# Feed-forward product turned by a DMA instead of by TensorE, in a quantised attention and feed-forward kernel

## The chip, the cores and the metric

The kernel runs on one core of a Trainium2 chip. The metric is the device time of one execution in microseconds (us). A core has five engines with instruction streams of their own: PE (TensorE, matrix products into PSUM banks), DVE (VectorE), ACT (ScalarE), POOL (GpSimd) and SP (SyncE, which here only issues DMAs). Sixteen DMA engines move data between DRAM and SBUF. The engines wait for one another through semaphores, and each works through its own stream in order.

## The reference

Input x and a context, both [64, 128, 256] in float32, go through four residual layers: a gated-memory attention, a ternary linear layer, a softmax cross-attention, and a quantised feed-forward layer. Only the last is touched. For each row of 256 values:

```python
def _act_quant(x):
    scale = 127.0 / clip(max(abs(x), axis=-1), 1e-5)
    return clip(round(x * scale), -128, 127) / scale
def _bitlinear(x, w):                       # w: ternary weights times their mean
    return einsum('bsi,oi->bso', _act_quant(x), _weight_quant(w))
gate = silu(_bitlinear(x, w_gate))          # 256 -> 1024
up = _bitlinear(x, w_up)                    # 256 -> 1024
x = x + _bitlinear(gate * up, w_down)       # 1024 -> 256
```

So the product `gate * up` (128 rows by 1024 of a block) has to be scaled by its row's maximum, rounded to whole numbers up to 127, and turned so that the 1024 inner values lie on the partitions, where the last matrix product sums over them.

## The kernel before

The batch is 64 blocks of 128 rows, in 16 groups (`NG`) of four. The first three layers run as a software pipeline over the groups, whose order is written out by hand in `turn` and `schedule`; the change doesn't touch it. The feed-forward layer follows as a stage of its own over the 64 blocks, with loops unrolled in the program and an order by hand: `ffn_turn` on each engine says what it does for which block in which turn. Its input rows were quantised earlier, stored to DRAM (`rows_q`), and come back turned: SP issues one transposing DMA for each block (`rows_turned`, 128 rows by 256 in bf16), four blocks ahead, as soon as the up product of a block is in its bank.

In turn i of that stage:

- PE makes the gate and up products of block i (`gate_up`, 8 matmuls of 512 columns), turns the rounded product of block i-2 (`product_rows`, 8 transposes), and makes the down product of block i-3 (`down`, 8 matmuls of 256 columns).
- ACT takes silu of the gate banks (`silu`), copies the turned product of block i-2 from PSUM to `fhT` (`product_t`), and scales the down product of block i-3 (`scale_out`).
- DVE multiplies up and silu (`ffn_mul`, the tile `C`), takes the row maximum (`hmax`), guards and scales it (`hstep7`), and inverts it (`hscale`).
- POOL makes the factor for the way back (`scale_back`), rounds the product by adding a large constant (`ffn_round`, tile `wtmp`; the whole number then stands in the low 16 bits), and adds the residual (`ffn_out`).
- SP issues `rows_turned` of block i+4, and for every group one store of 512 KB and one load of 512 KB.

Beside this, `last_rows` on ACT, DVE and POOL normalises and quantises the input rows of the last groups during turns 1 to 46.

Of the kernel before, what the change touches and what calls it, by code (L numbers as in the profile page):

```python
# [5 lines left out]
P = 128  # L6
B = 64
E = 256
# [3 lines left out]
GB = 4  # L12
NG = B // GB
INNER = 1024
# [8 lines left out]
OFFSET = 1536.0  # L23
CODE = 8388608.0 + 0x6600

# [89 lines left out]
def build(nc, x, ctx_in, ig_w, ig_b, fg_w, fg_b, out_w, w0, wq, wkv, w_gate, w_up, w_down, out):  # L115
    rows_q = nc.dram_tensor("rows_q", [B, P, E], BF16, kind="Internal").ap()
    with ExitStack() as ctx:
# [179 lines left out]
        fh = flat(C).rearrange("p (i n) -> p i n", i=2)  # L297
        fhr = flat(wtmp).rearrange("p (i n) -> p i n", i=2)
        fhr_low = fhr.bitcast(F16).rearrange("p i (n w) -> p i n w", w=2)[:, :, :, 0]
# [3 lines left out]
        hstep7 = sb("hstep7", [P, FB])  # L303
        hscale = sb("hscale", [P, FB])
        hback = sb("hback", [P, FB])
# [13 lines left out]
        f_hstep = sem("f_hstep")  # L319
# [8 lines left out]
        h_full, h_clear = sem("h_full"), sem("h_clear")  # L328
# [11 lines left out]
        bank_h = [ps[k].bitcast(F16) for k in (7, 0)]  # L340
# [17 lines left out]

        def feed_forward(eng, turn, behind={}):

            for g in range(NG):
                turn(g, g % 4, g == 0, g == NG - 1)
                if g in behind:
                    behind[g]()


        @block.sync
        def _(sp):
# [58 lines left out]
            def rows_written(g):  # L427

                def wait():
                    sp.wait_ge(q_out, 16 * (g + 1) + 16)  # L430
                return wait

            def written():
                sp.wait_ge(x_out, 16 * NG)

            def turn(g, p, first, last):
                for s in range(FB):
                    i = FB * g + s
                    if not last:
                        hold("sp", sp, u_full, i + 1)  # L440
                        rows_turned(i + FB, s)
                    if s == FB - 1 and not first:
                        sp.wait_ge(f_done, FB * g)
                        sp.dma_start(grp(out, g - 1), fo[(p + 1) % 2][:, :, :]).then_inc(f_out[(p + 1) % 2], 16)
                        if g + 3 < NG:
                            q = (p + 3) % 4
                            sp.dma_start(fx[q], grp(out, g + 3)).then_inc(f_in[q], 16)

            feed_forward(sp, turn, {NG - 7: written, NG - 5: rows_written(NG - 3), NG - 4: rows_written(NG - 2),
                                    NG - 3: rows_written(NG - 1)})  # L450
            sp.wait_ge(f_done, B)
            sp.dma_start(grp(out, NG - 1), fo[1][:, :, :]).then_inc(f_out[1], 16)
# [5 lines left out]
        def _(pe):  # L458
# [212 lines left out]
            def product_rows(i, s):  # L671
                pe.wait_ge(f_hr, i + 1)
                pe.wait_ge(h_clear, i + 1)
                for c in range(IC):
                    mm = pe.transpose(bank_h[s % 2][:, c * P:(c + 1) * P], fhr_low[:, s % 2, c * P:(c + 1) * P], ident_h[:, :])  # L675
                mm.then_inc(h_full, 1)

            def down(i, s):
                pe.wait_ge(o_clear, i + 1)
                o = bank_o[s % 2]  # L680
                pe.wait_ge(h_clear, i + 3)
                for c in range(IC):
                    mm = pe.matmul(o[:, 0:E], fhT[:, s % 2, c * P:(c + 1) * P], WD[:, c, :],  # L683
                                   start=(c == 0), stop=(c == IC - 1))
                mm.then_inc(o_full, 1)
# [12 lines left out]
            def ffn_turn(g, p, first, last):  # L698
                for s in range(FB):
                    i = FB * g + s  # L700
                    if i > 0:
                        gate_up(i, s, g)
                    if i == 2:
                        pe.wait_ge(x3_ready, GB * NG)
                    if s > 1 or not first:
                        product_rows(i - 2, s + 2)
                    if s > 2 or not first:
                        down(i - 3, s + 1)

            feed_forward(pe, ffn_turn)  # L710
            product_rows(B - 2, 2)
            down(B - 3, 1)
            product_rows(B - 1, 3)
            down(B - 2, 2)
            down(B - 1, 3)


        @block.scalar
        def _(act):
# [233 lines left out]
            def product_t(i, s):  # L953
                act.wait_ge(h_full, i + 1)
                act.activation(fhT[:, s % 2, :], bank_h[s % 2], ACT.Copy, bias=-OFFSET).then_inc(h_clear, 1)  # L955

            def scale_out(i, s):
                act.wait_ge(f_hback, i + 1)
                act.wait_ge(o_full, i + 1)
                if not isinstance(i, int) or i > 1:  # L960
                    act.wait_ge(f_done, i - 1)
                act.activation(fy[:, s % 2, :], bank_o[s % 2][:, 0:E], ACT.Identity,
                               scale=hback[:, s % FB:s % FB + 1]).then_inc(o_clear, 1)


            def ffn_turn(g, p, first, last):
                for s in range(FB):
                    i = FB * g + s
                    silu(i, s, g, p % 2)
                    if s > 1 or not first:  # L970
                        product_t(i - 2, s + 2)
                    if s > 2 or not first:
                        scale_out(i - 3, s + 1)
                    last_rows(i)

            feed_forward(act, ffn_turn)
            product_t(B - 2, 2)
            scale_out(B - 3, 1)
            product_t(B - 1, 3)
            scale_out(B - 2, 2)  # L980
            scale_out(B - 1, 3)


        @block.gpsimd
        def _(pool):
# [112 lines left out]
            def scale_back(i, s):  # L1098
                if not isinstance(i, int) or i > 3:
                    pool.wait_ge(o_clear, i - 1)  # L1100
                hold("pool", pool, f_hstep, i + 1)
                pool.tensor_scalar(hback[:, s % FB:s % FB + 1], hstep7[:, s % FB:s % FB + 1], mean_abs[:, 3:4], 1.0,  # L1102
                                   ALU.mult, ALU.mult).then_inc(f_hback, 1)

            def ffn_round(i, s):
                if not isinstance(i, int) or i > 1:
                    pool.wait_ge(h_full, i - 1)
                hold("pool", pool, f_hs, i + 1)
                pool.tensor_scalar(fhr[:, s % 2, :], fh[:, s % 2, :], hscale[:, s % FB:s % FB + 1], CODE,  # L1109
                                   ALU.mult, ALU.add).then_inc(f_hr, 1)  # L1110

            def ffn_out(i, s, g, p):
                if s == 0:
                    pool.wait_ge(f_out[p % 2], 8 * (g - p % 2) + 16)
                    pool.wait_ge(f_in[p], 4 * (g - p) + 16)
                pool.wait_ge(o_clear, i + 3)
                pool.tensor_tensor(fo[p % 2][:, s, :], fy[:, s % 2, :], fx[p][:, s, :], ALU.add).then_inc(f_done, 1)

            def ffn_turn(g, p, first, last):
                for s in range(FB):  # L1120
                    i = FB * g + s
                    scale_back(i, s)
                    ffn_round(i, s)
                    if s > 2:
                        ffn_out(i - 3, s - 3, g, p)
                    elif not first:
                        ffn_out(i - 3, s + 1, g - 1, (p - 1) % 4)
                    last_rows(i)

            feed_forward(pool, ffn_turn)  # L1130
            for s in range(1, FB):
                ffn_out(B - FB + s, s, NG - 1, 3)
# [3 lines left out]
        def _(dve):  # L1136
# [3 lines left out]
            for freed, spare in ((g_clear, 1), (u_clear, 1), (h_clear, 2), (o_clear, 2)):  # L1140
                dve.sem_inc(freed, spare)
# [321 lines left out]
            def ffn_mul(i, s, g, p):  # L1463
# [4 lines left out]
                if not isinstance(i, int) or i > 1:  # L1468
                    dve.wait_ge(f_hr, i - 1)
                dve.scalar_tensor_tensor(out=fh[:, s % 2, :], in0=up, scalar=fback[:, p, s % FB, 1:2],  # L1470
                                         in1=fsil[:, s % 2, :], op0=ALU.mult, op1=ALU.mult).then_inc(u_clear, 1)
                dve.wait_ge(u_clear, i + 2)
                dve.tensor_reduce(hmax[:, s % FB:s % FB + 1], fh[:, s % 2, :], AX.X, ALU.max,  # L1473
                                  apply_absolute_value=True).then_inc(f_hm, 1)

            def row_scale(i, s):
                dve.wait_ge(f_hm, i + 1)
                if not isinstance(i, int) or i > 3:
                    dve.wait_ge(f_hback, i - 3)
# [42 lines left out]
```

## Time and profile before

| | us |
|---|---|
| median of 3 runs | 706.99 (706.68 to 709.64) |
| profiled execution | 705.16 |
| its span, first to last instruction | 703.2 |
| busy in the span: PE, DVE, ACT, POOL | 663.5, 616.5, 512.4, 378.8 |
| mean granted TensorE clock | 0.993 of full speed |
| DMA traffic | 55.52 MB, 72657 packets |

Times in the profile count from the start of the span. Busy time leaves out register, branch, semaphore and DMA-issuing instructions; those of SP stand in the timeline under SPq, with the time for which issuing held the queue. A busy PE is not PE at its peak, since matmuls overlap and their ends are modelled; the distance between two starts is the better measure.

### The profile page before, as it was taken

How to read it: one execution, taken by the hardware profiler on the slowest of the kernel's cores; microseconds unless marked ns; L12 is line 12 of the kernel's file. 1: busy time of each engine (PE TensorE's matmuls, PEld its weight loads, DVE VectorE, ACT ScalarE, POOL GpSimd, SP SyncE). 2: the span in 40 equal slices, each digit the busy share in tenths (PEclk: the TensorE clock that was granted, in tenths of full speed). 3: DMA queues.
4: the chain of work that ended last, by engine and by line, in shares of the span. 5: the costliest groups of instructions: out<-in, count | busy, mean ns of one | idle time of the engine just before them, and what ended most of it. 6: DMA issues, size and time to landing. Idle time of an engine off the chain costs nothing.

```text
span 703.2 us, 15197 instructions
## 1 busy us (share of the span) xinstructions
PE 663.5 (94%) x4942; PEld 511.3 (73%) x4942; DVE 616.5 (88%) x1660; ACT 512.4 (73%) x1171; POOL 378.8 (54%) x554
## 2 busy tenths in 40 slices
PE   4888999999999999999999999998899999999996
PEld 3677887877978879788787797876465665666664
DVE  4698798898898988989889889887999999999994
ACT  3456676777768777787777776865588888888885
POOL 2264554734645537355464473552366667666665
PEclk9999999999999999999999999999999999999999
DMA  8202023031220221212202121014123423435221
GB/s 302 89 1 61 7 85 91 16 91 46 76 91 16 91 80 42 91 30 92 93 15 92 49 73 61 16 56 155 50 84 95 143 79 115 122 83 158 80 81 60
DMA packets 72657, 55.52 MB, mean 79 GB/s; under 512 B 20093, under 2 KB 72318, under 8 KB 72582
## 3 DMA queue, kind: packets, MB, share of 16 engines
q1 hardware_dynamic: 64134, 50.37, 23.0%
q10 hardware_dynamic: 8448, 4.20, 2.1%
q8 instruction: 41, 0.67, 0.4%
q14 instruction: 34, 0.28, 0.1%
HBM read 29.39 MB, written 20.97 MB: 72 GB/s over the span
## 4 chain that ended last, share of the span: by engine, by line
PE 65%; DVE 22%; ACT 8%; issue 2%; DMA 1%; POOL 1%; POOLq 0%; DVEq 0%; ACTq 0%
PE bank L666 11%; PE bank L585 9%; PE bank L634 8%; PE bank L615 7%; PE bank L683 5%; PE bank L655 4%; DVE C L1470 4%; ACT ew L822 4%; PE bank L491 4%; DVE hmax L1473 4%; PE bank L554 3%; PE bank L588 3%; PE bank L675 3%; PE bank L627 2%; PE bank L545 2%
## 5 line engine op out<-in xcount | busy, mean ns | idle before, releaser
L666 PE MATMUL bank<-WGU,fqT 128*128 128x512 bf16 x512 | 125.0, 382 | 4.8 <-DVE C L1470 4.4
L1034 POOL TENSOR_SCALAR_AFFINE_SELECT D<-D 128x512 f32<-128x512 f32 x64 | 38.3, 636 | 157.9 <-ACT D L813 157.9
L666 PEld LDWEIGHTS bank<-WGU,fqT 128*128 128x128 bf16 x512 | 48.1, 98 | 57.7 <-DVE C L1470 17.9
L1470 DVE SCALAR_TENSOR_TENSOR C<-bank,fback,D 128x1024 f32<-128x1024 f32 x64 | 81.9, 1279 | 7.4 <-ACT D L951 5.9
L1019 POOL TENSOR_TENSOR rs<-ve,minus_half 128x4 f32<-128x4 f32 x64 | 65.1, 1025 | 35.9 <-DVE ve L1163 35.7
L951 ACT ACTIVATE D<-bank,fback 128x1024 f32<-128x1024 f32 x64 | 71.1, 1110 | 15.9 <-PE bank L666 15.9
L955 ACT ACTIVATE fhT<-bank 128x1024 f16<-128x1024 f16 x64 | 65.5, 1023 | 20.4 <-PE bank L675 19.1
L1473 DVE TENSOR_REDUCE hmax<-C 128x1 f32<-128x1024 f32 x64 | 78.1, 1220 | 2.2
L585 PE MATMUL bank<-WX,qcT 128*128 128x268 f32 x256 | 74.0, 412 | 0.0
L1109 POOL TENSOR_SCALAR wtmp<-C,hscale 128x1024 f32<-128x1024 f32 x64 | 71.6, 1119 | 0.2 <-issue 0.2
L683 PE MATMUL bank<-WD,fhT 128*128 128x256 f16 x512 | 66.4, 273 | 0.3 <-ACT fhT L955 0.3
L1157 DVE BATCH_NORM_STATS2 st<-x 128x6 f32<-128x256 f32 x180 | 63.1, 412 | 2.6
L615 PEld LDWEIGHTS bank<-vaug,C 128*128 128x128 f32 x512 | 61.6, 194 | 2.6 <-issue 1.9
L615 PE MATMUL bank<-vaug,C 128*128 128x65 f32 x512 | 61.6, 274 | 1.5 <-DVE C L1263 1.5
L554 PE MATMUL bank<-qcT,GT 128*128 128x512 f32 x128 | 60.2, 594 | 0.7 <-ACT GT L906 0.7
L634 PE MATMUL bank<-W0T,x1T 128*128 128x256 f32 x256 | 59.4, 385 | 0.0
L1102 POOL TENSOR_SCALAR hback<-hstep,mean_abs 128x1 f32<-128x1 f32 x64 | 17.2, 268 | 77.1 <-DVE hscale L1483 65.1
L1046 POOL TENSOR_TENSOR hr<-hv,minus_half 128x16 f32<-128x16 f32 x16 | 47.4, 2960 | 17.6 <-DVE hv L1292 17.6
L634 PEld LDWEIGHTS bank<-W0T,x1T 128*128 128x128 f32 x256 | 47.3, 190 | 9.0 <-DVE C L1263 3.0
L869 ACT ACTIVATE qn<-xg,shift,rs 128x256 f32<-128x256 f32 x64 | 33.2, 589 | 27.9 <-POOL shift L1026 27.9
L1040 POOL TENSOR_TENSOR hh<-us,head_scale 128x256 f32<-128x256 f32 x64 | 45.0, 724 | 13.9 <-ACT usq L808 13.9
L683 PEld LDWEIGHTS bank<-WD,fhT 128*128 128x128 f16 x512 | 47.4, 98 | 4.9 <-issue 0.6
(191 smaller groups left out, 1557.9 us busy)
## 6 DMA issues: line engine op xcount, KB each, us to landing
out_dram<-x SPq DMA_DIRECT2D x31, 512.0 KB, 3.1
xg<-in_x_dram SPq DMA_DIRECT2D x16, 512.0 KB, 3.9
cg<-in_ctx_dram SPq DMA_DIRECT2D x16, 512.0 KB, 4.5
rows_q<-fq ACTq DMA_DIRECT2D x16, 256.0 KB, 2.3
xg<-out_dram SPq DMA_DIRECT2D x8, 512.0 KB, 4.4
cg<-out_dram SPq DMA_DIRECT2D x8, 512.0 KB, 4.6
raw<-in_L_ffn_w_gate_dram SPq DMA_DIRECT2D x1, 1024.0 KB, 8.1
x<-in_L_ffn_w_up_dram SPq DMA_DIRECT2D x1, 1024.0 KB, 10.1
```

Of the source, the lines that this page charges most:

```text
L554: mm = pe.matmul(o[:, :], GT[:, c, rows_at * P:(rows_at + 1) * P], turned[:, EC + c, :, :].rearrange("p b t -> p (b t)"), start=(c == 0), ...
L585: pe.matmul(o[:, 0:VG], qcT[p][:, EC + c, b, :], WX[:, c, :], start=(c == 0), stop=False, skip_group_check=True)
L615: mm = pe.matmul(o[:, h * AUG:(h + 1) * AUG], C[:, b, h, :], vaug[q][:, b, h, :], start=True, stop=True)
L634: mm = pe.matmul(o[:, 0:E], x1T[:, b, c * P:(c + 1) * P], W0T[:, c, :], start=(c == 0), stop=(c == EC - 1))
L666: mm = pe.matmul(ps[k + half], fqT[:, s, c, :], WGU[:, c, which, half * 512:(half + 1) * 512], start=(c == 0), stop=(c == EC - 1))
L683: mm = pe.matmul(o[:, 0:E], fhT[:, s % 2, c * P:(c + 1) * P], WD[:, c, :], start=(c == 0), stop=(c == IC - 1))
L951: act.activation(fsil[:, s % 2, :], gate, ACT.Silu, scale=fback[:, p, s % FB, 0:1]).then_inc(g_clear, 1)
L955: act.activation(fhT[:, s % 2, :], bank_h[s % 2], ACT.Copy, bias=-OFFSET).then_inc(h_clear, 1)
L1019: pool.tensor_tensor(rs[i][:, :], ve[i][:, :], minus_half[:, 0:GB], ALU.pow).then_inc(rstd[i], 1)
L1109: pool.tensor_scalar(fhr[:, s % 2, :], fh[:, s % 2, :], hscale[:, s % FB:s % FB + 1], CODE, ALU.mult, ALU.add).then_inc(f_hr, 1)
L1470: dve.scalar_tensor_tensor(out=fh[:, s % 2, :], in0=up, scalar=fback[:, p, s % FB, 1:2], in1=fsil[:, s % 2, :], op0=ALU.mult, op1=ALU.mult ...
L1473: dve.tensor_reduce(hmax[:, s % FB:s % FB + 1], fh[:, s % 2, :], AX.X, ALU.max, apply_absolute_value=True).then_inc(f_hm, 1)
```

## The change

1. `product_rows` on PE and `product_t` on ACT are gone, with their two banks. In their place ACT turns the rounded product of block i-2 into whole numbers in f16 in SBUF (`whole_products`, tile `fw`), SP stores them to a DRAM tensor `rows_h` (`product_stored`, 256 KB), and SP issues a transposing DMA of the 128 by 1024 tile from `rows_h` into one of three tiles (`product_turned`).
2. `down` runs five blocks behind `gate_up` instead of three; `scale_out` and `ffn_out` run six behind.
3. The guard of the maximum (1e-5) is written once into a 1025th column of the product's tile, so the maximum itself is guarded; the DVE instruction that made `hstep7` is gone. DVE inverts the maximum directly, and POOL makes both the factor 127/max and the factor for the way back.
4. SP's loop is written anew: in turn i it issues `rows_turned` of block i+4, `product_turned` of block i-3, `product_stored` of block i-2, and in every fourth turn the group's store and load.

The core of the diff:

```diff
+    rows_h = nc.dram_tensor("rows_h", [4, P, INNER], F16, kind="Internal").ap()
-        fh = flat(C).rearrange("p (i n) -> p i n", i=2)
+        fh = [flat(vg[k])[:, 0:INNER + 1] for k in (1, 2)]
+        fw = flat(usq).bitcast(F16).rearrange("p (i n) -> p i n", i=2)
+        turned = [fhT[:, 0, :], fhT[:, 1, :], flat(us).bitcast(F16)[:, 0:INNER]]
 # SP
+            def group_out(g):
+                sp.wait_ge(f_done, FB * g + FB)
+                sp.dma_start(grp(out, g), fo[g % 2][:, :, :]).then_inc(f_out[g % 2], 16)
+                if g + 4 < NG:
+                    sp.dma_start(fx[g % 4], grp(out, g + 4)).then_inc(f_in[g % 4], 16)
+            def product_stored(i):
+                sp.wait_ge(f_w, i + 1)
+                if i > 3:
+                    sp.wait_ge(h_turned[(i - 4) % 3], 16 * ((i - 4) // 3) + 16)
+                sp.dma_start(rows_h[i % 4, :, :], fw[:, i % 2, :]).then_inc(h_stored[i % 2], 16)
+            def product_turned(i):
+                hold("sp", sp, h_stored[i % 2], 16 * (i // 2) + 16)
+                if i > 2:
+                    hold("sp", sp, o_full, i - 2)
+                sp.dma_start_transpose(turned[i % 3].rearrange("p (c t) -> p c t", c=IC),
+                                       rows_h[i % 4, :, :]).then_inc(h_turned[i % 3], 16)
+            def ffn_block(i):
+                if i + FB < B:
+                    hold("sp", sp, u_full, i + 1)
+                    rows_turned(i + FB, i % FB)
+                if i > 2:
+                    product_turned(i - 3)
+                if i > 1:
+                    product_stored(i - 2)
+                if i % FB == 2 and i > 2 * FB:
+                    group_out(i // FB - 2)
 # PE
-            def product_rows(i, s):
...
+            def down(i):
+                pe.wait_ge(o_clear, i + 1)
+                o = bank_o[i % 2]
+                pe.wait_ge(h_turned[i % 3], 16 * (i // 3) + 16)
 # ACT
-                act.activation(fhT[:, s % 2, :], bank_h[s % 2], ACT.Copy, bias=-OFFSET).then_inc(h_clear, 1)
+            def whole_products(i):
+                act.wait_ge(f_hr, i + 1)
+                if i > 1:
+                    act.wait_ge(h_stored[i % 2], 16 * ((i - 2) // 2) + 16)
+                act.activation(fw[:, i % 2, :], fhr[:, i % 2, :], ACT.Copy, bias=-CODE).then_inc(f_w, 1)
 # POOL
+                pool.tensor_scalar(hscale[:, s:s + 1], hinv[:, s:s + 1], 127.0, None, ALU.mult).then_inc(f_hs, 1)
...
+                pool.tensor_scalar(hback[:, k:k + 1], hmax[:, s:s + 1], mean_abs[:, 3:4], 1.0 / 127.0,
                                    ALU.mult, ALU.mult).then_inc(f_hback, 1)
 # DVE
-                dve.tensor_scalar(hstep7[:, s % FB:s % FB + 1], hmax[:, s % FB:s % FB + 1], Q_EPS, 1.0 / 127.0,
-                                  ALU.max, ALU.mult).then_inc(f_hstep, 1)
+                dve.reciprocal(hinv[:, s:s + 1], hmax[:, s:s + 1]).then_inc(f_hinv, 1)
+            for k in range(2):
+                dve.memset(fh[k][:, INNER:INNER + 1], Q_EPS).then_inc(f_guard, 1)
```

## Rows read from the trace of the kernel before

**Rows 1.** Multiply of the feed-forward stage, one per block: duration min/median/max, first and last start.
```profile
L1470 DVE SCALAR_TENSOR_TENSOR C<-bank,fback,D x64: 1266/1283/1285, 492.5 to 691.3; 128x1024 f32<-128x1024 f32 x64
```

**Rows 2.** Windows: length, busy time of each engine, granted clock, DMA share, GB/s.
```profile
496.00:497.00 1.00, 0.26 (x2) 0.00 (x0) 1.00 (x4) 0.70 (x1) 0.80 (x1) 1.00 0.00 0
497.00:498.00 1.00, 0.00 (x0) 0.00 (x0) 0.79 (x2) 0.41 (x1) 0.00 (x0) 1.00 0.00 0
498.00:499.00 1.00, 0.25 (x1) 0.13 (x2) 0.96 (x2) 0.00 (x0) 0.00 (x0) 0.64 0.81 272
499.00:500.00 1.00, 1.00 (x3) 0.30 (x2) 0.97 (x2) 0.00 (x0) 0.00 (x0) 0.50 1.01 290
...
502.00:503.00 1.00, 1.00 (x6) 0.41 (x5) 1.00 (x1) 0.99 (x2) 0.00 (x0) 1.00 0.29 66
...
556.00:600.00 44.00, 43.03 (x334) 27.08 (x333) 42.23 (x76) 37.53 (x48) 29.15 (x45) 1.00 0.40 120
```

**Rows 3.** Timeline of one block's period: start, length, engine, line.
```profile
602.23 1.28 DVE L1470 SCALAR_TENSOR_TENSOR C<-bank,fback,D 128x1024 f32<-128x1024 f32 x1
...
602.97 1.89 PE L666 MATMUL bank<-WGU,fqT 128*128 128x512 bf16 x8
...
604.70 0.61 PE L675 MATMUL bank<-ident_h,wtmp 128*128 128x128 f16 x8
604.80 0.15 DVE L1480 TENSOR_SCALAR hstep<-hmax 128x1 f32<-128x1 f32 x1
604.99 0.16 DVE L1483 RECIPROCAL hscale<-hstep 128x1 f32<-128x1 f32 x1
...
605.14 1.04 PE L683 MATMUL bank<-WD,fhT 128*128 128x256 f16 x8
...
605.27 1.28 DVE L1470 SCALAR_TENSOR_TENSOR C<-bank,fback,D 128x1024 f32<-128x1024 f32 x1
...
606.01 1.89 PE L666 MATMUL bank<-WGU,fqT 128*128 128x512 bf16 x8
```

**Rows 4.** Groups of instructions, 497 to 690 us: shapes and count, then busy us and mean ns.
```profile
L1473 DVE TENSOR_REDUCE hmax<-C 128x1 f32<-128x1024 f32 x62 | 75.7, 1220 | 2.1
L1109 POOL TENSOR_SCALAR wtmp<-C,hscale 128x1024 f32<-128x1024 f32 x61 | 68.3, 1119 | 0.2 <-issue 0.2
L951 ACT ACTIVATE D<-bank,fback 128x1024 f32<-128x1024 f32 x61 | 67.7, 1110 | 13.9 <-PE bank L666 13.9
L955 ACT ACTIVATE fhT<-bank 128x1024 f16<-128x1024 f16 x61 | 62.4, 1023 | 18.1 <-PE bank L675 16.8
L962 ACT ACTIVATE nrm<-bank,hback 128x256 f32<-128x256 f32 x60 | 28.4, 474 | 0.0
L1117 POOL TENSOR_TENSOR x<-nrm,xg 128x256 f32<-128x256 f32 x32 | 23.2, 725 | 0.0
L1102 POOL TENSOR_SCALAR hback<-hstep,mean_abs 128x1 f32<-128x1 f32 x61 | 16.4, 268 | 66.6 <-DVE hscale L1483 63.1 <-DVE hstep L1480 3.5
L1483 DVE RECIPROCAL hscale<-hstep 128x1 f32<-128x1 f32 x61 | 10.0, 164 | 2.1
L1480 DVE TENSOR_SCALAR hstep<-hmax 128x1 f32<-128x1 f32 x61 | 9.4, 154 | 2.1
L756 ACT ACTIVATE fq<-raw 128x1024 bf16<-128x1024 f32 x3 | 3.1, 1045 | 0.0
```

**Rows 5.** Issues on the queues by line: ns min/median/max, first and last start.
```profile
L414 SPq DMA_TRANSPOSE fqT<-rows_q x64: 1167/1170/2117, 470.4 to 678.8; - x64
L444 SPq DMA_DIRECT2D out_dram<-x x15: 372/372/378, 518.4 to 693.2; - x15
L447 SPq DMA_DIRECT2D xg<-out_dram x6: 501/502/510, 518.8 to 632.7; - x6
L760 ACTq DMA_DIRECT2D rows_q<-fq x16: 378/379/431, 131.1 to 640.3; - x16
```

**Rows 6.** SP's queue in order of time: first issue of the stage's loop, then 555 to 560.
```profile
497.79 6.86 SPq L414 DMA_TRANSPOSE fqT<-rows_q  x4
...
556.39 0.37 SPq L444 DMA_DIRECT2D out_dram<-x  x1
556.82 1.58 SPq L447 DMA_DIRECT2D cg<-out_dram  x1
558.51 1.17 SPq L414 DMA_TRANSPOSE fqT<-rows_q  x1
```

**Rows 7.** DMA issues: KB each, median us from issue to landing.
```profile
rows_q<-fq ACTq DMA_DIRECT2D x16, 256.0 KB, 2.3
fqT<-rows_q SPq DMA_TRANSPOSE x64, 2.4
```

**Rows 8.** The last store, from the timeline of the end.
```profile
699.87 0.37 SPq L452 DMA_DIRECT2D out_dram<-x  x1
```

**Rows 9.** DMA, 505 to 517 us (four transposing DMAs); then queue 10, whole span.
```profile
q1 hardware_dynamic: 990, 0.22, 8.2%
...
q10 hardware_dynamic: 8448, 4.20, 2.1%
```

**Rows 10.** One issue of the small transposing DMA, then windows of 0.1 us.
```profile
470.44 1.28 SPq L414 DMA_TRANSPOSE fqT<-rows_q  x1
...
471.70:471.80 0.10, 0.00 (x0) 0.00 (x0) 0.10 (x1) 0.00 (x0) 0.00 (x0) 1.00 0.00 0
471.80:471.90 0.10, 0.00 (x0) 0.00 (x0) 0.07 (x2) 0.00 (x0) 0.00 (x0) 1.00 0.24 59
...
472.00:472.10 0.10, 0.00 (x0) 0.00 (x0) 0.10 (x2) 0.00 (x0) 0.00 (x0) 1.00 1.03 241
...
472.30:472.40 0.10, 0.00 (x0) 0.00 (x0) 0.10 (x2) 0.00 (x0) 0.10 (x1) 1.00 0.07 3
```

More of the change, by code:

```diff
@@ L318, in build @@
         f_hm = sem("f_hm")
-        f_hstep = sem("f_hstep")
+        f_w = sem("f_w")
+        f_guard = sem("f_guard")
+        f_hinv = sem("f_hinv")
+        h_turned = [sem(f"h_turned{s}") for s in range(3)]
+        h_stored = [sem(f"h_stored{s}") for s in range(2)]
         f_hs = sem("f_hs")
@@ L425, in _ @@
             sp.dma_start(grp(out, NG - 1), x3_last[:, :, :]).then_inc(x_out, 16)
[L427 to L447, printed above, removed]
@@ new lines, in ffn_block @@
+            def ffn_block(i):
[8 more added lines that the diff above has]
+                    group_out(i // FB - 2)
+            for i in range(B):
+                if i == FB * (NG - 6):
+                    sp.wait_ge(x_out, 16 * NG)
+                for g in range(NG - 3, NG):
+                    if i == FB * (g - 1):
+                        sp.wait_ge(q_out, 16 * (g + 1) + 16)
+                ffn_block(i)
@@ L453, in _ @@
+            product_turned(B - 3)
+            product_stored(B - 2)
+            product_turned(B - 2)
+            product_stored(B - 1)
+            product_turned(B - 1)
+            group_out(NG - 2)
+            group_out(NG - 1)
             for p in range(2):
@@ L669, in gate_up @@
                     mm.then_inc(full_k, 1)
[L671 to L673 removed]
+            def down(i):
+                pe.wait_ge(o_clear, i + 1)
+                o = bank_o[i % 2]
+                pe.wait_ge(h_turned[i % 3], 16 * (i // 3) + 16)
                 for c in range(IC):
[L675 to L683, printed above, removed]
+                    mm = pe.matmul(o[:, 0:E], turned[i % 3][:, c * P:(c + 1) * P], WD[:, c, :],
                                    start=(c == 0), stop=(c == IC - 1))
@@ L696, in _ @@
             turn(aft.part("O"), None, None, NG - 1, None, None, 1, (NG + 1) % 3)
[L698 to L715, printed above, removed]
+            for i in range(B):
+                if i > 0:
+                    gate_up(i, i % FB, i // FB)
+                if i == DEPTH:
+                    pe.wait_ge(x3_ready, GB * NG)
+                if i >= DEPTH:
+                    down(i - DEPTH)
+            for i in range(B - DEPTH, B):
+                down(i)
         @block.scalar
@@ L951, in silu, with scale_out @@
                 act.activation(fsil[:, s % 2, :], gate, ACT.Silu, scale=fback[:, p, s % FB, 0:1]).then_inc(g_clear, 1)
-            def product_t(i, s):
-                act.wait_ge(h_full, i + 1)
-                act.activation(fhT[:, s % 2, :], bank_h[s % 2], ACT.Copy, bias=-OFFSET).then_inc(h_clear, 1)
-            def scale_out(i, s):
+            def whole_products(i):
[3 more added lines that the diff above has]
+                act.activation(fw[:, i % 2, :], fhr[:, i % 2, :], ACT.Copy, bias=-CODE).then_inc(f_w, 1)
+            def scale_out(i):
                 act.wait_ge(f_hback, i + 1)
                 act.wait_ge(o_full, i + 1)
-                if not isinstance(i, int) or i > 1:
+                if i > 1:
                     act.wait_ge(f_done, i - 1)
[L962 to L981, printed above, removed]
+                act.activation(fy[:, i % 2, :], bank_o[i % 2][:, 0:E], ACT.Identity,
+                               scale=hback[:, i % (2 * FB):i % (2 * FB) + 1]).then_inc(o_clear, 1)
+            for i in range(B):
+                silu(i, i % FB, i // FB, i // FB % 2)
+                if i > 1:
+                    whole_products(i - 2)
+                if i > DEPTH:
+                    scale_out(i - DEPTH - 1)
+                last_rows(i)
+            whole_products(B - 2)
+            scale_out(B - DEPTH - 1)
+            whole_products(B - 1)
+            for i in range(B - DEPTH, B):
+                scale_out(i)
         @block.gpsimd
@@ L1116, in ffn_out @@
                 pool.wait_ge(o_clear, i + 3)
[L1117 to L1128, printed above, removed]
@@ L1130, in _ @@
-            feed_forward(pool, ffn_turn)
-            for s in range(1, FB):
-                ffn_out(B - FB + s, s, NG - 1, 3)
+                pool.tensor_tensor(fo[g % 2][:, s, :], fy[:, i % 2, :], fx[g % 4][:, s, :], ALU.add).then_inc(f_done, 1)
+            for i in range(B):
+                product_scales(i)
+                ffn_round(i)
+                if i > DEPTH:
+                    ffn_out(i - DEPTH - 1)
+                last_rows(i)
+            for i in range(B - DEPTH - 1, B):
+                ffn_out(i)
@@ L1485, in ffn_turn @@
-            def ffn_turn(g, p, first, last):
-                for s in range(FB):
-                    i = FB * g + s
-                    ffn_mul(i, s, g, p % 2)
-                    row_scale(i, s)
-                    if s == 1 and not last:
-                        scales(g + 1, 1 - p % 2)
-                    last_rows(i)
-            feed_forward(dve, ffn_turn)
+                dve.reciprocal(hinv[:, s:s + 1], hmax[:, s:s + 1]).then_inc(f_hinv, 1)
+            for k in range(2):
+                dve.memset(fh[k][:, INNER:INNER + 1], Q_EPS).then_inc(f_guard, 1)
@@ L1498 @@
+            for i in range(B):
+                ffn_mul(i)
+                if i % FB == 1 and i < B - FB:
+                    scales(i // FB + 1, (i // FB + 1) % 2)
+                last_rows(i)
 _INS = ['x', 'ctx_1024', 'L0_xattn_igate_w', 'L0_xattn_igate_b', 'L0_xattn_fgate_w', 'L0_xattn_fgate_b',
```

67 lines of the change are left out of this document (28 added, 39 removed).

## Prediction

> **What bounds the kernel now.** Only the feed-forward stage is touched, so I looked for its pace first. The multiply L1470 runs once a block, from 492.5 to 691.3 us [rows 1]: 198.8 us for 63 periods, 3.16 us each. The windows show two engines nearly full there, PE 43.03 and DVE 42.23 of 44 us at a granted clock of 1.00 [rows 2]. The timeline says why [rows 3]. By starts, PE spends 604.70 - 602.97 = 1.73 us on gate and up, 605.14 - 604.70 = 0.44 on the eight transposes and 606.01 - 605.14 = 0.87 on down: 3.04, back to back. DVE's period beside it is 605.27 - 602.23 = 3.04 as well, of which 1.28 + 1.22 + 0.15 + 0.16 = 2.81 are the four steps of the block [rows 1, 4]; the turns with extra work of `last_rows` stretch the mean to 3.16. PE and DVE set the pace together. ACT needs 1.11 + 1.02 + 0.47 = 2.60 a block, POOL 0.27 + 1.12 + 0.73 = 2.12 [rows 4]. The engine that hardly shows in the busy table is SP: its queue is held for 1.17 us by each transposing DMA, 0.37 us by a store and 0.50 us by a load of 512 KB [rows 5]. Today that is 1.17 + (0.37 + 0.50)/4 = 1.39 us of 3.16.
>
> **The change, part by part.**
>
> PE loses the transposes: 0.44 us a block, 3.04 to 2.60. DVE loses `hstep7` with its gap: 604.99 - 604.80 = 0.19 [rows 3], 3.04 to 2.85; a 1025th column is 1.22/1024, nothing. ACT trades a copy of 1.02 us out of PSUM for one out of SBUF; the nearest row of that shape is `fq<-raw`, 1.05 [rows 4], so +0.02, 2.62. POOL gains a second one-column operation of 0.27: 2.39 a block. If no more were changed, DVE would set the pace, and 63 x 0.19 = 12 us would go.
>
> What is added stands on SP's queue, in each turn: `rows_turned` (as now), `product_turned`, `product_stored`, and in every fourth turn store and load of a group.
>
> *Issue of `product_turned`.* The trace has no transposing DMA of 128 x 1024, only of 128 x 256. Lower bound: issuing costs the same whatever the size, 1.17 us. Upper bound: it grows wholly with the size, 4 x 1.17 = 4.68 us. A plain load holds the queue 0.50 us and a plain store 0.37 for eight times the bytes of that transposing one [rows 5], so the plain part of an issue is about (0.50 + 0.37)/2 = 0.44 us, and the other 0.73 us belong to the transposing. I take that the 0.73 grow with the tiles: 0.44 + 4 x 0.73 = 3.36 us.
>
> *Issue of `product_stored`.* The 256 KB store on ACT's queue holds it for 0.38 us, the 512 KB one on SP's 0.37 [rows 5]; with a gap of 0.06 to the next issue [rows 6] I take 0.43.
>
> *The new wait.* `product_turned(i-3)` waits until the store of block i-3 has landed, and that store was the last thing SP issued in the turn before. A 256 KB store lands 2.3 us after its issue [rows 7]. Between lie 0.43 us of its own issue and `rows_turned`, 1.17 + 0.10 for the gap of a held issue (558.51 - 556.82 - 1.58 = 0.11) [rows 6]: SP stands still for 2.3 - 0.43 - 1.27 = 0.60 us. Behind it on SP wait the next `product_stored`, the next `rows_turned` and the group's output; so everything waits. The turn after a group's store and load is spared (0.43 + 0.55 > 0.60), 13 of them; from turn 60 on there is no `rows_turned`, and the wait is 1.87.
>
> A turn of SP is thus 1.27 + 0.60 + 3.46 + 0.43 + (0.43 + 0.55)/4 = 6.0 us, against 2.85 for the next slowest engine. The sum over the stage:
>
> - `rows_turned` 60 x 1.27 = 76.2
> - `product_turned` 64 x 3.46 = 221.4
> - `product_stored` 64 x 0.43 = 27.5
> - group stores 16 x 0.43 and loads 12 x 0.55 = 13.5
> - waits 44 x 0.60 + 7 x 1.87 - 0.4 = 39.1
>
> 377.7 us in all, from 497.8, where SP's loop starts [rows 6]: 875.5. At its start SP waits some 2 us for the first whole product. The end: landing after the last issue 2.4 - 1.17 = 1.2 [rows 7], down 0.9, `scale_out` 0.5, `ffn_out` 0.7, the last store until the span's end 703.2 - 699.87 = 3.3 [rows 8], gaps 0.2, less the 0.9 of group stores counted already: 5.9. PE, idle for some 3 us of each turn, won't keep its clock: after the stretch from 496 to 499, in which it was busy 0.51 us, the granted clock was 0.50 of full, 1.2 GHz, and 1.00 again from 502 [rows 2]. At half the clock gate, up and down are 5.2 us a turn, still under 6.0, so this costs only 0.9 more in the last down product. The span is 875.5 + 2 + 5.9 + 0.9 = 884.3, and with the 705.16 - 703.2 = 2.0 us around it the profiled execution takes 886. The median of the runs before lies 1.8 us above the profiled one; I forecast 887.
>
> *Is the DMA itself a limit?* Four transposing DMAs took 8.2% of 16 engines in 12 us [rows 9], 15.7 engine-us or 0.25 us of all sixteen each; four times that is 0.98 a block. The 16 stores of 256 KB took 2.1% of the span on queue 10 [rows 9], 0.92 us of all sixteen each. With the 0.40 share of today's 3.16 us [rows 2], 1.26, that is 3.2 us a block: hidden under SP's 6.0, but no longer under a pace of 2.85.
>
> **The rivals.**
>
> *Flat issue.* A transposing DMA of four times the size holds SP no longer than 1.17. For it: the packets of a small one come in a burst of some 0.5 us that begins as its issue ends, not spread over the issue [rows 10]. Then 64 x 2.19 = 140 us less than the sum: 746. It still is slower, since the wait for the store stays and SP's turn is 3.7. Against it: plain issues of far more bytes are shorter, so the shape must cost something. The Trainium skill (Advanced Engine Details and Errata, X-Bar Transpose (TRN2)) says that transposing DMAs are as fast as regular ones, at 350 to 400 GB/s. By that rule alone, 256 KB would be moved in about 0.7 us (an estimate from that page), and this rival would be the right one. The trace agrees for the packets, 0.25 us of all sixteen engines for 64 KB, but not for the issue, three times as long as a plain store's.
>
> *Wholly proportional issue.* 4.68 instead of 3.36: 64 x 1.32 = 84 us more, 971. For it: nothing in the trace separates the fixed part. Against it: the fixed part of plain issues.
>
> *SP keeps up.* The issue is flat and the store lands while SP does other work, so the wait is nothing. SP's turn is then 1.27 + 1.27 + 0.43 + 0.25 = 3.2, and the DMA engines' 3.2 lies beside it: no change, 706. If both stay under DVE's pace, the 12 us come through, less a longer drain: after the last multiply came 703.2 - 691.3 = 11.9 us, and the new chain of multiply, maximum, inverse, scale, round, copy, store, turn, down, scale, add and output is 1.28 + 1.22 + 0.16 + 0.27 + 1.12 + 1.05 + 2.3 + 2.4 + 0.87 + 0.47 + 0.73 + 3.3 = 15.2, 3.3 more. That gives 705.2 - 12 + 3.3 = 697 to 698. It decides at an SP turn of under 3.0 us, which asks for an issue shorter than that of the tile a quarter as large.
>
> **How the numbers follow.** The forecast, with an issue between 2.6 and 3.9 us and so 840 to 925, has 0.62; flat or nearly so (742 to 800) 0.17; proportional 0.11; SP keeps up 0.10, of it 0.06 faster (697) and 0.04 no change (706). No measurable change means within 0.5%, 703.5 to 710.5. The likeliest case alone would have 840 to 925. The range for 8 in 10 takes in the flat case and leaves out the proportional one and the two fast ones: 742 to 940. Faster 0.06, same 0.04, slower 0.90.
>
> **What would show it.** In the changed profile: issues of the 128 x 1024 transposing DMA of about 3.4 us on SP's queue; the queue idle only for the store's landing, about 0.6 us a turn, and never for the up product; PE's idle time ended by the DMA into `fhT` and `us`, or by the one into `fqT`; a granted clock with stretches of 0.50; periods of the multiply near 6 us; PE's, DVE's and ACT's busy time per block as worked out above. The prediction is wrong if that issue is near 1.2 us, if SP waits for engines and not they for it, or if the DMA share is near 1 (then the packets are the limit and not the issuing).

## The result and the profile after

The changed kernel takes 802.3 us (median of 4, 801.7 to 803.2) against 706.8 before (median of 4): a ratio of 1.135, 95% interval 1.132 to 1.138. It is slower by 95 us. I had forecast 887 with a range of 742 to 940. The direction and the place (SP's queue) held; the size was off by 85 us, chiefly because one term of the sum, the issue of the large transposing DMA, was far too high. The time lies in the range, but not in the 840 to 925 of the likeliest case.

The page of the changed kernel, its span and chain, shows where the end is decided now. The columns of the first fence are engine, busy us, share, instructions.

```profile
span 800.0 us, 14423 instructions
...
PE 666.0 (83%) x4430; PEld 490.3 (61%) x4430; DVE 607.8 (76%) x1598; ACT 513.5 (64%) x1171; POOL 391.3 (49%) x618
...
DMA packets 149455, 89.03 MB, mean 111 GB/s; under 512 B 88701, under 2 KB 140926, under 8 KB 149382
...
PE 41%; DMA 18%; SPq 15%; DVE 14%; ACT 6%; issue 4%; POOL 1%; POOLq 0%; DVEq 0%; ACTq 0%
DMA rows_h<-usq 16%; SPq L439 9%; PE bank L599 8%; PE bank L648 7%; PE bank L629 7%; PE bank L669 3%; ACT ew L820 3%; PE bank L568 3%; SPq L410 3%; PE bank L505 3%; PE bank L602 3%; PE bank L559 2%; PE bank L641 2%; PE bank L550 2%; DVE rawmax L1290 2%
```

No engine has much more to do than before (PE 666.0 us busy against 663.5, DVE 607.8 against 616.5, ACT 513.5 against 512.4, POOL 391.3 against 378.8); PE, DVE and ACT just wait. The store of the product to DRAM (`rows_h<-usq`) and SP's issues stand in the chain. The multiply, now L1463, shows the pace (compare [rows 1]):

```profile
L1463 DVE SCALAR_TENSOR_TENSOR vg<-bank,fback,D x64: 1271/1284/1285, 495.7 to 772.6; 128x1024 f32<-128x1024 f32 x64
```

276.9 us for 63 periods is 4.40 us, against 3.16 before; 63 x 1.24 = 78 of the 95 us. The stage also starts 3 us later in this execution; the kernels below, whose first layers are the same, start it between 492.8 and 497.1, so that is scatter. The rest is a longer drain: from the last multiply to the end of the span 800.0 - 772.6 = 27.4 us against 11.9 before.

The issues on SP, by line: ns min/median/max (compare [rows 5]). L439 is `product_turned`, L433 `product_stored`, L410 `rows_turned`.

```profile
L439 SPq DMA_TRANSPOSE fhT<-rows_h x43: 1231/1232/2084, 507.2 to 790.2; - x43
DMA to landing us min/median/max: 3.0/3.3/5.1
...
L433 SPq DMA_DIRECT2D rows_h<-usq x64: 336/524/1302, 504.9 to 787.7; - x64
DMA to landing us min/median/max: 2.2/2.6/4.0
...
L410 SPq DMA_TRANSPOSE fqT<-rows_q x64: 1167/1187/1905, 472.1 to 760.4; - x64
```

Here is the term that failed: the transposing DMA of 128 x 1024 holds SP's queue for 1.232 us, hardly more than the 1.17 of the tile a quarter as large. I had taken 3.36.

SP's queue in order of time, two turns:

```profile
641.10 0.53 SPq L433 DMA_DIRECT2D rows_h<-usq  x1
641.73 1.18 SPq L410 DMA_TRANSPOSE fqT<-rows_q  x1
644.07 1.23 SPq L439 DMA_TRANSPOSE fhT<-rows_h  x1
645.40 0.52 SPq L433 DMA_DIRECT2D rows_h<-usq  x1
646.03 1.18 SPq L410 DMA_TRANSPOSE fqT<-rows_q  x1
648.08 1.23 SPq L439 DMA_TRANSPOSE fhT<-rows_h  x1
```

From 641.10, the issue of a store, to 645.40, the next one, are 4.30 us. The transposing DMA can't go before that store has landed, and the next store can't go before the transposing DMA, in SP's order. So a turn is the store's landing plus one issue, and `rows_turned` lies inside the landing. The waits of SP's queue over the whole execution say the same (us in total, times, longest; L341 is the helper `hold`, in which SP waits ahead of a transposing DMA):

```profile
SPq L341 <- DMA rows_h<-usq: 53.7, 50, 2.2
```

Everyone else waits for what comes out of this ring, and PE no longer keeps its clock (windows: length, busy PE, PEld, DVE, ACT, POOL, granted clock, DMA share, GB/s; compare [rows 2]):

```profile
600.00:650.00 50.00, 35.07 (x176) 18.05 (x176) 31.25 (x45) 31.34 (x42) 24.87 (x47) 0.90 0.70 179
...
792.00:800.00 8.00, 1.86 (x8) 1.02 (x8) 0.00 (x0) 0.52 (x2) 1.44 (x2) 0.50 0.48 154
```

### The profile page after: what moved, and what is told of

The parts are those of the page before. It is cut to its first block, busy times and chain, and to the rows that moved or that the text cites. A ratio compares the mean times of both kernels' runs of the same rounds, so it can differ in the third digit from the quotient of the medians.

```text
span 800.0 us, 14423 instructions
## 1 busy us (share of the span) xinstructions
PE 666.0 (83%) x4430; PEld 490.3 (61%) x4430; DVE 607.8 (76%) x1598; ACT 513.5 (64%) x1171; POOL 391.3 (49%) x618
## 4 chain that ended last, share of the span: by engine, by line
PE 41%; DMA 18%; SPq 15%; DVE 14%; ACT 6%; issue 4%; POOL 1%; POOLq 0%; DVEq 0%; ACTq 0%
DMA rows_h<-usq 16%; SPq L439 9%; PE bank L599 8%; PE bank L648 7%; PE bank L629 7%; PE bank L669 3%; ACT ew L820 3%; PE bank L568 3%; SPq L410 3%; PE bank L505 3%; PE bank L602 3%; PE bank L559 2%; PE bank L641 2%; PE bank L550 2%; DVE rawmax L1290 2%
## 5 line engine op out<-in xcount | busy, mean ns | idle before, releaser
L1463 DVE SCALAR_TENSOR_TENSOR vg<-bank,fback,D 128x1024 f32<-128x1024 f32 x64 | 82.1, 1283 | 96.5 <-PE bank L680 46.6
L680 PE MATMUL bank<-WGU,fqT 128*128 128x512 bf16 x512 | 133.0, 405 | 6.3 <-DVE vg L1463 6.0
L955 ACT ACTIVATE usq<-wtmp 128x1024 f16<-128x1024 f32 x64 | 67.6, 1056 | 102.9 <-DMA rows_h<-usq 100.5
L690 PE MATMUL bank<-WD,fhT 128*128 128x256 f16 x344 | 50.3, 295 | 60.4 <-DMA fhT<-rows_h 60.4
L680 PEld LDWEIGHTS bank<-WGU,fqT 128*128 128x128 bf16 x512 | 52.3, 104 | 64.5 <-issue 13.4
L690 PEld LDWEIGHTS bank<-WD,fhT 128*128 128x128 f16 x344 | 33.2, 104 | 84.4 <-issue 78.5
L1014 POOL TENSOR_TENSOR rs<-ve,minus_half 128x4 f32<-128x4 f32 x64 | 65.2, 1026 | 38.3 <-DVE ve L1155 38.2
L1470 DVE TENSOR_REDUCE hmax<-vg 128x1 f32<-128x1025 f32 x64 | 78.1, 1221 | 2.2
L1106 POOL TENSOR_SCALAR wtmp<-vg,hscale 128x1024 f32<-128x1024 f32 x64 | 71.6, 1119 | 14.0 <-ACT usq L955 9.3
L1096 POOL TENSOR_SCALAR hscale<-hinv 128x1 f32<-128x1 f32 x64 | 13.6, 213 | 130.2 <-DVE hinv L1473 129.5
L690 PE MATMUL bank<-WD,us 128*128 128x256 f16 x168 | 26.0, 307 | 36.5 <-DMA us<-rows_h 36.5
```

What stands on the lines that cost most here:

```text
L680: mm = pe.matmul(ps[k + half], fqT[:, s, c, :], WGU[:, c, which, half * 512:(half + 1) * 512], start=(c == 0), stop=(c == EC - 1))
L690: mm = pe.matmul(o[:, 0:E], turned[i % 3][:, c * P:(c + 1) * P], WD[:, c, :], start=(c == 0), stop=(c == IC - 1))
L955: act.activation(fw[:, i % 2, :], fhr[:, i % 2, :], ACT.Copy, bias=-CODE).then_inc(f_w, 1)
L1106: pool.tensor_scalar(fhr[:, i % 2, :], fh[i % 2][:, 0:INNER], hscale[:, i % FB:i % FB + 1], CODE, ALU.mult, ALU.add).then_inc(f_hr, 1)
L1463: dve.scalar_tensor_tensor(out=fh[i % 2][:, 0:INNER], in0=up, scalar=fback[:, g % 2, s, 1:2], in1=fsil[:, i % 2, :], op0=ALU.mult, op1=ALU ...
L1470: dve.tensor_reduce(hmax[:, s:s + 1], fh[i % 2], AX.X, ALU.max, apply_absolute_value=True).then_inc(f_hm, 1)
```

## The experiments

The diffs are shortened to what matters, with comments of mine. Ratios are to the kernel before, run on the same chip. e3, e5, e6 and e7 leave out part of the work and compute other numbers than the reference; they serve for their times alone. "Period" is the mean distance of the multiply's starts over the 63 periods.

**e1: turn one turn later.** What sets the pace: the order on SP's queue, or full DMA engines?

```diff
-DEPTH = 5
+DEPTH = 6
-                if i > 2:
-                    product_turned(i - 3)
+                if i > 3:
+                    product_turned(i - 4)
```

(The group's output moves from turn 2 to turn 3 of four, for the later `ffn_out`.)

> The product is turned one turn later (block i-4 instead of i-3 in turn i), down six behind instead of five; same DMAs, same bytes. Theory (order on SP's queue): in the changed kernel a turn of SP is the store's issue to landing, 2.6 to 3.0 us, then 1.33 for the transposing issue, 4.4 a turn in all; here the store has a whole turn more to land, SP's turn is its issues 1.27 + 1.33 + 0.62 + 0.27 = 3.5 us, so about 64 x 0.9 = 58 us less than 802: 740 to 750. Rival (the DMA engines are full, share 0.73 and more in bursts, the order doesn't matter): within 10 us of 802.

757.2 us, ratio 1.072 (1.065 to 1.079): 45 us of the 95 come back for the same bytes and issues. The waits on SP's queue over the whole execution (first) and the DMA share (second, columns as above):

```profile
SPq L341 <- DMA rows_h<-usq: 1.4, 3, 0.8
```
```profile
600.00:650.00 50.00, 36.85 (x192) 18.73 (x193) 36.00 (x52) 32.12 (x42) 29.92 (x54) 0.93 0.94 223
```

The wait for the landing falls from 53.7 us to 1.4, and the time by 45. That the order sets the pace in the changed kernel is shown. The period is 3.77, not the 3.5 of the sum, and the DMA engines' share is 0.94 in this stretch: with the wait gone, the next limit is close. So the theory's number was missed by 7 us on the rival's side, and 50 us over the kernel before remain.

**e2: the store on ACT's queue.** `product_stored` moves, word for word, from SP to the end of ACT's turn.

```diff
-                if i > 1:
-                    product_stored(i - 2)          # SP
+                if i > 1:
+                    product_stored(i - 2)          # ACT, after scale_out
```

> The product's store is issued on ACT's queue, at the end of ACT's turn; all else as in the changed kernel. Theory (order on SP's queue): SP's turn loses the store's issue and the wait for its landing, 1.27 + 1.33 + 0.27 = 2.9 us; ACT's turn becomes 1.11 + 1.06 + 0.47 + 0.45 = 3.1 plus the extra rows, the DMA engines' 3.2: a period of 3.3 to 3.6 and 725 to 745. The store's landing from issue falls to about 2.3, since its packets no longer stand behind the turned tile's in one queue. Rival (DMA engines full): about 800, with landings as long as now.

760.6 us, ratio 1.074 (1.068 to 1.079), period 3.95. SP's wait for the landing is down from 53.7 to 10.9 us, but two things of the theory were wrong. The gain is 42 us and not 57 or more, and the landing became longer (DMA issues from 600 to 700 us: KB each, median us to landing):

```profile
rows_h<-usq ACTq DMA_DIRECT2D x23, 256.0 KB, 3.7
...
fqT<-rows_q SPq DMA_TRANSPOSE x23, 4.0
```

A queue of its own didn't shield the store from the packets of others; all landings grew, at a DMA share of 0.78 to 0.94. Instead SP now waits for the up product, which stands behind the down product on PE, which waits for the turned tile (PE 47.5 us from 520 to 740 us; below SP's waits, whole execution):

```profile
SPq L341 <- PE bank L670: 35.0, 15, 4.0
SPq L341 <- DMA rows_h<-usq: 10.9, 13, 1.7
```

The landings on this path were up to 6.9 us long. The Trainium skill (DMA: Bandwidth & Descriptors, Rules for kernel authors) says that spreading DMAs over issuing engines brings no bandwidth and only saves issue time; the trace agrees: SP's queue has 9% of the chain instead of 15%, and from 520 to 740 us 208 GB/s were moved, where e1 moved 223 with SP's queue alone. Why the store lands later here than in e1, where the DMA engines were at least as full (0.89 there, 0.85 here from 520 to 740 us, medians 2.8 and 3.6), is not shown.

**e7: half the product, order unchanged.** Only 512 of 1024 columns are stored and turned; down reads the same half twice.

```diff
-                sp.dma_start(rows_h[i % 4, :, :], fw[:, i % 2, :])...
+                sp.dma_start(rows_h[i % 4, :, :], fw[:, i % 2, 0:INNER // 2])...
-                sp.dma_start_transpose(turned[i % 3]...
+                sp.dma_start_transpose(turned[i % 3][:, 0:INNER // 2]...
```

> The changed kernel with only 512 of 1024 columns stored and turned, order as in the changed kernel; down reads the same half twice. Theory (the turn is the store's landing plus one transposing issue, the landing is 2.6 to 3.0 because of the packets ahead of it, and the issue costs 1.2 whatever the size): issue stays at 1.2, the landing falls to about 2.3, the turn from 4.4 to 3.9, 765 to 775. If the issue did grow with the size it would be near 0.7 and the time under 745. Rival (landing is fixed time and not packets): 795 to 802.

759.0 us, ratio 1.072 (1.068 to 1.077), period 3.80; 6 us under the range. Issues and landing:

```profile
L439 SPq DMA_TRANSPOSE fhT<-rows_h x43: 1188/1189/1976, 506.1 to 748.8; - x43
```
```profile
rows_h<-usq SPq DMA_DIRECT2D x64, 128.0 KB, 2.0
```

The issue of a transposing DMA is 1.17 us at 256 columns, 1.19 at 512 and 1.23 at 1024. The landing fell to 2.0, more than expected, and the turn by 0.60, the same 0.6 as the landing (2.6 to 2.0).

**e6: half the product and one turn later.** The two edits of e1 and e7 together.

```diff
+    product_turned(i - 4), DEPTH = 6               # as e1
+    512 of 1024 columns stored and turned          # as e7
```

> As e1_turn_later (product turned one turn later), but only 512 of the 1024 columns are stored and turned; down reads the same half twice. The number of issues on SP is the same, the product's bytes and packets are halved. Theory (in e1 the DMA engines are the limit: share 0.86 to 0.94 at a turn of 3.9 us, while SP's issues sum to 3.5): a turn of about 3.5 us, bounded by SP's issues, 725 to 735. Rival (SP's issues are already the limit in e1): no change, 750 to 757.

741.3 us, ratio 1.050 (1.045 to 1.055), period 3.60: 16 us under e1, so packets held e1 back, and 6 over the range. SP's queue waited for hardly anything from 520 to 720 us:

```profile
SPq L433 <- ACT usq L956: 1.9, 4, 0.6
SPq L341 <- PE bank L681: 0.5, 1, 0.5
```

Its issues with their gaps are the whole turn of 3.6 us, where I had summed 3.5. In e1 the same issues were longer by 9 us in all (`product_turned` 81.6 us against 78.0, of which 64 x 0.043 = 2.8 are the larger tile; `rows_turned` 80.6 against 76.5; `product_stored` 37.0 against 35.6), and SP's waits from 540 to 730 us 7.9 instead of 2.4: together 15 of the 16 us. So with the landing out of the way the limit is SP's issuing, and the packets add to it; both theories named half of it.

**e8: one more issue.** The same 1024 columns in two transposing DMAs.

```diff
-                sp.dma_start_transpose(turned[i % 3]..., rows_h[i % 4, :, :])
+                for k in range(2):
+                    part = slice(k * (INNER // 2), (k + 1) * (INNER // 2))
+                    sp.dma_start_transpose(turned[i % 3][:, part]..., rows_h[i % 4, :, part])
```

> The changed kernel with the product turned by two transposing DMAs of 512 columns instead of one of 1024: same bytes, same waits, one more issue a turn. Theory (an issue costs the same whatever its size, and it stands in SP's chain): 1.2 us more a turn, 64 x 1.2 = 77 us, about 880. Rival (issue time goes with the size, each half then costs half): 802 to 810.

862.3 us, ratio 1.219 (1.215 to 1.223), period 5.27.

```profile
L441 SPq DMA_TRANSPOSE fhT<-rows_h x86: 1188/1259/1737, 507.4 to 851.8; - x86
```

Each half costs a whole issue, 1.26 us. The time grows by 60 us where the theory gave 77; the store's median landing is 2.4 instead of 2.6 here, and SP waits 38.2 us for it instead of 53.7, which makes up for 15 us of the difference. If issue time went with the size, nothing would have been added.

**e3: no DMAs of the product.** What would the engines take without them? Store and transposing DMA are left out, and ACT writes straight into the tile that down reads.

```diff
-                if i > 1:
-                    act.wait_ge(h_stored[i % 2], 16 * ((i - 2) // 2) + 16)
-                act.activation(fw[:, i % 2, :], fhr[:, i % 2, :], ACT.Copy, bias=-CODE).then_inc(f_w, 1)
+                if i > 2:
+                    act.wait_ge(o_full, i - 2)
+                act.activation(turned[i % 3], fhr[:, i % 2, :], ACT.Copy, bias=-CODE).then_inc(f_w, 1)
```

> Store and transposing DMA of the product are left out: ACT writes the whole numbers straight into the tile that down reads, unturned, so the down product is of other numbers. All the work of PE, DVE, ACT and POOL of the changed kernel stays. Theory: without the two DMAs DVE sets the pace at 2.85 to 2.95 us a turn, and the time is 690 to 700, 12 us or so under the kernel before. Rival (the engines' own new order, down five behind and the two small operations on POOL, costs something too): over 707.

710.4 us, ratio 1.004 (1.002 to 1.007), period 3.11. By its number the rival had won. But the waits from 520 to 690 us (us in total, times, longest) show ACT standing before its copy for a down product:

```profile
ACT fhT L933 <- PE bank L668: 16.4, 33, 1.1
...
ACT us L933 <- PE bank L668: 7.8, 14, 1.2
```

With three tiles and down five behind, ACT's copy of block i has to wait for down of block i-3, made in the same turn. The changed kernel has no such wait; I had added it.

**e5: the same without that wait.** ACT writes its own pair of tiles and down reads `fhT` as it stands. The diff is against e3.

```diff
-                if i > 2:
-                    act.wait_ge(o_full, i - 2)
-                act.activation(turned[i % 3], fhr[:, i % 2, :], ACT.Copy, bias=-CODE).then_inc(f_w, 1)
+                act.activation(fw[:, i % 2, :], fhr[:, i % 2, :], ACT.Copy, bias=-CODE).then_inc(f_w, 1)
```

> As e3_no_dma (no store, no transposing DMA of the product), but ACT writes the whole numbers into its own pair of tiles and down reads fhT as it stands, so ACT no longer waits for a down product to free its tile, a wait that e3 had added. Down is of other numbers. Theory: that added wait (24 us of ACT in the stage) is what hid the gain in e3, and the engines' own work takes 690 to 700. Rival (ACT's three steps with the extra rows, 2.64 plus 0.6, and the handing to and fro of banks between PE, ACT and DVE set 3.1 us anyway): 703 to 710.

695.0 us, ratio 0.984 (0.980 to 0.989), period 2.92.

```profile
520.00:680.00 160.00, 152.27 (x891) 82.18 (x890) 153.50 (x216) 145.26 (x190) 128.74 (x230) 1.00 0.39 112
```

DVE sets the pace at 153.5 of 160 us: its own waits there come to 2 us, and PE waits 39 us for it. So the engines' side of the change is worth the 12 us of the prediction, and the two DMAs with their waits cost 802.3 - 695.0 = 107 us.

**e4 and e10: the guard column alone.** The kernel before, with only the guard as a 1025th column and both scales on POOL; PE turns the product. e10 is the same kernel, timed again beside e9.

```diff
-                dve.tensor_scalar(hstep7[...], hmax[...], Q_EPS, 1.0 / 127.0, ALU.max, ALU.mult).then_inc(f_hstep, 1)
-                dve.reciprocal(hscale[...], hstep7[...]).then_inc(f_hs, 1)
+                dve.reciprocal(hinv[...], hmax[...]).then_inc(f_hinv, 1)
+                pool.tensor_scalar(hscale[...], hinv[...], 127.0, None, ALU.mult).then_inc(f_hs, 1)
```

> The kernel before with only the guard as a 1025th column and both scales on POOL; the product is still turned by PE. Theory: PE's 3.04 us a block stays, DVE's falls by 0.19 to 2.85; only turns in which DVE was longer than PE (extra rows, mean period 3.16) gain, up to (3.16 - 3.04) x 63 = 7 us: 700 to 704. Rival (PE and DVE wait for one another through the banks, so nothing comes through, or POOL's second small operation lies on the way to the rounding): 706 to 709.

> e4_guard_alone once more, beside e9 on the same chip, to have its ratio with a narrower interval: 702 to 705, ratio 0.993 to 0.997. If the first result was chance, the interval reaches 1.

704.2 us, ratio 0.995 (0.993 to 0.997), and 705.3, ratio 0.997 (0.995 to 0.998). In e4's profile PE is now the only full engine:

```profile
520.00:600.00 80.00, 79.05 (x613) 51.74 (x623) 73.86 (x112) 71.79 (x94) 61.59 (x111) 1.00 0.42 121
```

Its period is 3.09. Both intervals lie under 1, at 0.3 to 0.5%: a small gain, at the upper edge of what I had expected, and the only version here that computes the reference and beats both kernels.

**e9: half the blocks by DMA.** The numbers so far said that SP and the DMA engines have room for half the product. Odd blocks go through DRAM, even ones through PE; down takes them in the order 0, 2, 1, 4, 3 and so on.

```diff
+                if i > 3 and i % 2 == 0:
+                    product_turned(i - 3)
+                if i > 2 and i % 2:
+                    product_stored(i - 2)
+                if i > 1:                              # ACT
+                    (whole_products if i % 2 else product_t)(i - 2)
```

> Blocks of odd number are turned by store and transposing DMA, those of even number by PE's transposes and ACT's copy as in the kernel before; guard column as in the changed kernel; down products in the order 0, 2, 1, 4, 3, 6, 5 and so on, so that a DMA-turned block has two turns more. Theory: SP's turn is 1.27 + (1.33 + 0.62)/2 + 0.25 = 2.5 us with the landing hidden, PE's 2.60 + 0.22 = 2.82, DVE's 2.85: no queue is over DVE's pace, and the time comes near that of e5_no_dma_free (695), with PE's uneven turns (3.04 and 2.60) costing some of it: 696 to 701, faster than the kernel before and than the guard alone. Rival (any product sent through DRAM puts SP's landing wait or the DMA engines' load on the path): over 707.

728.2 us, ratio 1.030 (1.027 to 1.033): a clear miss, on the rival's side. Its SP queue:

```profile
624.46 0.51 SPq L441 DMA_DIRECT2D cg<-out_dram  x1
625.09 1.59 SPq L424 DMA_TRANSPOSE fqT<-rows_q  x1
626.79 0.52 SPq L448 DMA_DIRECT2D rows_h<-usq  x1
627.43 1.18 SPq L424 DMA_TRANSPOSE fqT<-rows_q  x1
631.88 1.23 SPq L455 DMA_TRANSPOSE fhT<-rows_h  x1
```

In the group's turn the product's store stands behind 1 MB of the group's load and store; the transposing DMA can go only 5 us after that store's issue, and SP waits 29.5 us for landings from 520 to 700 us.

**e11: the group's load behind the product's store.**

```diff
+                if i % FB == 2 and i > 2 * FB:
+                    group_out(i // FB - 2)             # the store alone, ahead of product_turned
                 if i > 3 and i % 2 == 0:
                     product_turned(i - 3)
                 if i > 2 and i % 2:
                     product_stored(i - 2)
-                if i % FB == 2 and i > 2 * FB:
-                    group_out(i // FB - 2)
+                if i % FB == 3 and i > 2 * FB:
+                    group_in(i // FB - 2)
```

> As e9_half_and_half, with SP's order in the group's turns changed: the group's 512 KB store is issued ahead of the transposing DMA of its turn, the 512 KB load only in the turn after, behind the product's store. Theory (in e9 SP stood still for up to 3.2 us in every fourth turn, 29.5 us in all, because the product's store had the group's load and store ahead of it in the DMA queue and landed 5 us after its issue): the landing is back near 3 us, SP waits under 10 us in all, 702 to 712. Rival (not the packets ahead of that store but the load of the DMA engines as such makes it late): 724 to 730 as in e9.

721.9 us, ratio 1.019 (1.015 to 1.023), between the theory's range and the rival's. SP's waits from 520 to 700 us:

```profile
SPq L439 <- POOL x L1161: 19.3, 13, 1.6
SPq L345 <- PE bank L698: 13.4, 19, 2.2
SPq L345 <- DMA rows_h<-usq: 4.0, 8, 1.9
```

The landing is as the theory said: its median from 560 to 700 us fell from 3.3 to 2.4, and the wait from 29.5 to 4.0. But by moving the group's store forward I had made SP wait for POOL's `ffn_out` of the same turn, 19.3 us, against 0.5 in e9, with the transposing DMA behind it, and down waiting for that. The number was missed. That this new wait is what holds the kernel at 722 is argued and not shown, and a mixed kernel under 704 stays untried.

## Why the prediction was right in direction and wrong in size

- *PE, DVE, ACT, POOL.* Right. e5 gives 695 for an engines' side that the prediction put 12 us under the kernel before, at a period of 2.92 for 2.85 plus the extra rows.
- *Issue of the transposing DMA.* This is the step that failed: "I take that the 0.73 grow with the tiles". The prediction itself had said that it is wrong if this issue is near 1.2 us, and it is. Measured is 1.23 at four times the size, and e7 and e8 show the same from both sides: half the size costs 1.19, two halves cost two issues. Over 64 turns 64 x (3.36 - 1.23) = 136 us too much; with gaps and some stretched issues the queue had 94 us where the sum had 221. The rival *flat issue*, to which I gave 0.17, is what happened in this term. The rule of the Trainium skill (Advanced Engine Details and Errata, X-Bar Transpose (TRN2)), that transposing DMAs are as fast as regular ones, speaks of moving the bytes and not of issuing. For the bytes the trace agrees in the comparison, but not with the 350 to 400 GB/s: by [rows 9] 64 KB in 0.25 us are 262 GB/s and a plain 256 KB store in 0.92 us is 285 (estimates from the shares). That the 1.17 us of the small tile were fixed, no row told.
- *The evidence I passed over.* The packets of a small transposing DMA came in one burst at the end of its issue [rows 10]. Had each tile cost issue time, they would have been spread over it. I named this for the rival and gave it too little weight.
- *Where luck comes in.* The forecast missed by 85 us and not by 127 because the other terms, all too small, gave 43 back. And 802 lies in the range because that was stretched down to 742 for the flat rival; the range of the likeliest case missed it.
- *The new wait.* Right in mechanism, as e1 shows, too small in size. I took the landing of a store on an idle machine, 2.3 us [rows 7]; under the new traffic it is 2.6 in the median and up to 4.0. SP waited 53.7 us instead of 39.1.
- *The other terms.* The product's store holds the queue 0.52 us and not 0.37: with gaps 41 us instead of 27.5. `rows_turned` with gaps came to 87 instead of 76, some of its issues being stretched to 1.9 behind a load. Summed over the timeline of SP's queue, from 500.75 to 791.45: 87 + 94 (turned, with gaps) + 41 + 14.5 (groups) + 53.7 (waits) = 290, where the prediction had 377.7.
- *The flat rival's own number*, 746, was 56 us too low in time for the same reasons (its turn adds up to 3.8 us, not the 3.7 written there, and 4.4 was measured): 15 for the wait, 14 for the store's issue, 13 for the turned issue (94 us with gaps and some stretched ones, for 64 x 1.27 = 81), 11 for `rows_turned`, 1 for the groups, and some 3 for the later start and the slower drain.
- *The DMA engines' load.* Right: a share of 0.69 over the 292 us from 500 to 792 is 3.15 us a block, for the 3.2 of the prediction. The packets grew with the bytes as summed, and the issue did not.
- *Clock.* Right and nearly harmless: granted 0.90 in a stretch of the stage, where PE is hardly in the chain (0.5% of it from 520 to 720 us), and 0.50 at the end. There the last down product took 1.86 us instead of the 1.04 of [rows 3], 0.8 more for the 0.9 of the prediction.
- *SP keeps up.* Excluded by every run that has the two DMAs in each turn: the fastest of them that moves all the bytes, e1, takes 757 us.

## What to carry to other kernels

Before moving work to a DMA, sum the issuing queue's turn: every issue, plus every wait for a landing that stands in the same in-order queue. A store and the read of the same data in one queue make a ring of landing plus issue; give the store a whole turn to land, as e1 did, before asking for more. And don't scale the price of an issue by the bytes without a row that shows it: count the issues first, then the bytes.

## What the hardware showed that I had not expected

- A transposing DMA holds SP's queue for 1.17, 1.19 and 1.23 us at 128 rows by 256, 512 and 1024 columns of two bytes; two of 512 columns cost 2 x 1.26. A plain 256 KB store holds it 0.52 here, and ACT's queue, which issues no transposing DMAs, 0.34 (e2).
- The landing of a 256 KB store on SP's queue grows slowly with what else the DMA engines carry: from 520 to 740 us its median is 2.4 us at a share of 0.57 (e8), 2.7 at 0.71 (the changed kernel) and 2.8 at 0.89 (e1). On ACT's queue it is 3.6 at 0.85 (e2), so on a queue of its own it landed later, not sooner. One behind 1 MB of other traffic took 5.1 us (e9), and half the size 2.0 at 0.57 (e7).
